# One-core graph network kernel: row moments on GpSimd, seven of eight tiles normalised on VectorE, and a reordered first row block

## The reference, cut to what matters

```
h  = relu(layernorm(x))
Wh = h @ W;  src = Wh @ a[:F];  dst = Wh @ a[F:]
att = softmax(where(adj > 0, leaky_relu(src + dst.T, 0.2), -9e15), axis=1)
x  = x + gru(att @ Wh, h)              # gates from w_ih, w_hh, b_ih, b_hh
h  = relu(layernorm(x))
out = x + adj @ (h @ W1.T + b1)
```

## Time and profile before

| | us |
|---|---|
| median of 3 runs | 1553.67 (1552.84 to 1554.71) |
| the profiled execution | 1554.47 |
| its span, first to last instruction | 1552.9 |
| TensorE busy | 1485.6 (96%) |
| VectorE busy | 1386.0 (89%) |
| ScalarE busy | 1369.6 (88%) |
| GpSimd busy | 136.2 (9%) |

### The profile page before, as it was taken

One profiled execution on the slowest core, in us unless ns is written; L12 is line 12 of the kernel. 1 busy time (PEld: TensorE's weight loads), 2 busy tenths in 40 slices (PEclk: granted clock), 3 DMA queues, 4 the chain that ended last, 5 costly groups with the idle time before them and its releaser, 6 DMA issues.

```text
span 1552.9 us, 35381 instructions
## 1 busy us (share of the span) xinstructions
PE 1485.6 (96%) x13262; PEld 1304.4 (84%) x13262; DVE 1386.0 (89%) x2256; ACT 1369.6 (88%) x1972; POOL 136.2 (9%) x98
## 2 busy tenths in 40 slices
PE   5477999999999999999999999999999999999998
PEld 5356888888888888888888888888888888888887
DVE  8997999999999999999999999997579877766684
ACT  5779999999999999999999999996185998777785
POOL 5000011001100010001000100010000000000000
PEclk9778999999999999999999999999999999999999
DMA  8858999999999999999999999996386999888860
GB/s 314 298 204 332 365 350 360 352 366 353 355 357 370 352 349 353 374 351 357 359 365 345 362 362 355 349 360 265 122 354 238 408 361 352 308 304 310 321 228 16
DMA packets 96380, 502.93 MB, mean 324 GB/s; under 512 B 9599, under 2 KB 38985, under 8 KB 75337
## 3 DMA queue, kind: packets, MB, share of 16 engines
q1 hardware_dynamic: 78328, 444.54, 76.1%
q10 hardware_dynamic: 18000, 57.74, 9.8%
HBM read 418.32 MB, written 83.92 MB: 323 GB/s over the span
## 4 chain that ended last, share of the span: by engine, by line
PE 92%; DVE 5%; ACT 1%; issue 1%; DMA 0%; POOL 0%; DVEq 0%; ACTq 0%
PE ACC L1014 57%; PE ACC L1104 29%; PE GP L1040 2%; PE GP L1043 2%; PE GQ L1061 1%; ACT M L506 1%; DVE M L659 1%; DVE JK L642 1%; DVE TB L733 1%; DVE AE L728 1%; DVE JK L728 1%; PE TG L1027 0%; PE TG L1050 0%; DVE JK L646 0%; DVE M L751 0%
## 5 line engine op out<-in xcount | busy, mean ns | idle before, releaser
L1014 PE MATMUL ACC<-TB,M 128*128 128x258 f16 x8192 | 927.2, 275 | 41.8 <-DVE M L751 30.7
L1014 PEld LDWEIGHTS ACC<-TB,M 128*128 128x128 fp8e4 x8192 | 804.5, 98 | 150.7 <-issue 43.2
L506 ACT ACTIVATE M<-SB,dsteep 128x256 fp8e4<-128x256 f32 x1273 | 526.2, 538 | 0.0
L516 ACT ACTIVATE JK<-X 128x3328 uint8<-128x3328 uint32 x124 | 373.2, 3010 | 0.0
L692 DVE TENSOR_SCALAR Y<-X 128x4096 fp8e4<-128x4096 f32 x128 | 291.9, 2280 | 5.9 <-DMA X<-in_adjb_dram 5.5
L605 ACT ACTIVATE TB<-TB 128x8192 uint8<-128x8192 fp8e4 x32 | 225.0, 7030 | 76.5 <-DVE TB L890 71.7
L1104 PE MATMUL ACC<-WG,X 128*128 128x256 f16 x2048 | 225.5, 273 | 0.0
L1104 PE MATMUL ACC<-WG,TB 128*128 128x256 f16 x2048 | 225.4, 273 | 0.0
L1104 PEld LDWEIGHTS ACC<-WG,X 128*128 128x128 fp8e4 x2048 | 200.4, 98 | 23.2
L1104 PEld LDWEIGHTS ACC<-WG,TB 128*128 128x128 fp8e4 x2048 | 200.4, 98 | 23.1
L743 DVE TENSOR_SCALAR M<-SB,nd 128x256 fp8e4<-128x256 f32 x775 | 213.7, 345 | 0.0
(11 more groups left out here) (145 smaller groups left out, 786.9 us busy)
## 6 DMA issues: line engine op xcount, KB each, us to landing
X<-in_adjb_dram SPq DMA_DIRECT2D x128, 2048.0 KB, 9.8
mask_bytes<-Y SPq DMA_DIRECT2D x128, 512.0 KB, 5.1
M<-in_adjb_dram ACTq DMA_DIRECT2D x24, 1920.0 KB, 9.8
X<-mask_bytes SPq DMA_DIRECT2D x16, 2048.0 KB, 9.5
TB<-mask_bytes SPq DMA_DIRECT2D x16, 2048.0 KB, 9.1
M<-in_adjb_dram ACTq DMA_DIRECT2D x4, 2048.0 KB, 11.9
M<-in_xb_dram SPq DMA_DIRECT2D x8, 512.0 KB, 8.3
h_rows<-M SPq DMA_DIRECT2D x8, 512.0 KB, 3.9
```

The costliest lines, as they stand in the source:

```text
L506: ins = nc.scalar.activation(rows(mask1(c), jj), SB[u][:, :], ACT.Sigmoid, scale=STEEP, bias=dsteep[:, j:j + 1], saturate=False)
L516: nc.scalar.activation(junk[:, 0:SEEN], X[c % 2][:, 0:SEEN].bitcast(u32), ACT.Sign, accum_out=nz[:, bass.ds(k, 1), at:at + 1].rearrange("p ...
L1014: ins = nc.tensor.matmul(A[t][m][:, 0:2 * TW], rows((mask1, mask2)[m](c), jj)[:, t * P:(t + 1) * P], TB[:, c * JC + jj, m, 0:2 * TW], star ...
```

## The change

Six edits, all at work before row block 1.

1. Row moments. VectorE aggregates only groups 0 and 1. For the others it runs `bn_stats` alone (`halves_stats`), and GpSimd's `pair_moments(p)` combines the two halves of each row's statistics for 16 tiles in seven small operations and raises to the power in an eighth. VectorE's order is now stats(0), stats(1), normalised(0), halves 2 and 3, the copy of `wext` that TensorE's first transposes wait for, normalised(1), halves 4 and 5, normalised(2), normalised(3), halves 6 and 7, normalised(4) to (7). GpSimd's pair 1 stands before the bias work, pairs 2 and 3 behind it.
2. BY_DVE is 7: VectorE normalises seven tiles of each group, ScalarE one.
3. GpSimd's weight work waits until VectorE has normalised everything (p_hd, 16).
4. X[0] is loaded after k = 11 and no longer after k = 7.
5. TSCALE goes into the exponent's bias as its logarithm; the two scalings (L720) fall away.
6. Row block 0. The low halves i = 3, 7, 11 and 15 are GpSimd's, with a semaphore t_lp of their own. ScalarE makes the first six comparisons (AHEAD) of the next part at the end of a part, so that behind the last high half of parts 1 to 3 only four comparisons stand and no longer ten.

The rest renumbers semaphores that are shared with these.

```diff
-BY_DVE = 6
+AHEAD = 6
+BY_DVE = 7
...
-                    if k in (7, 15):
+                    if k in (11, 15):
                         b = k // 15
                         sp.dma_start(X[b][:, :], adjb[b, :, :]).then_inc(c_in[b], 16)
...
+                def pair_moments(p):
...
+                    pool.wait_ge(p_st, 2 * p + 2)
+                    nc.gpsimd.tensor_tensor(px[0], mean_e, mean_o, ALU.add).then_inc(p_ag, 1)
+                    nc.gpsimd.tensor_tensor(px[1], part_e, part_o, ALU.add).then_inc(p_ag, 1)
+                    pool.wait_ge(p_ag, p * 6 - 5)
+                    nc.gpsimd.tensor_scalar(mean, px[0], 0.5, None, ALU.mult).then_inc(p_ag, 1)
+                    pool.wait_ge(p_ag, p * 6 - 4)
+                    nc.gpsimd.tensor_scalar(px[1], px[1], 1.0 / F, EPS, ALU.mult, ALU.add).then_inc(p_ag, 1)
+                    pool.wait_ge(p_ag, p * 6 - 3)
+                    nc.gpsimd.tensor_tensor(px[0], mean_e, mean, ALU.subtract).then_inc(p_ag, 1)
+                    pool.wait_ge(p_ag, p * 6 - 1)
+                    nc.gpsimd.tensor_tensor(px[0], px[0], px[0], ALU.mult).then_inc(p_ag, 1)
+                    pool.wait_ge(p_ag, p * 6)
+                    nc.gpsimd.tensor_tensor(sdx[:, at], px[1], px[0], ALU.add).then_inc(p_sd, 1)
+                    pool.wait_ge(p_sd, p + 2)
+                    nc.gpsimd.tensor_tensor(rsx[:, at], sdx[:, at], half[:, 0:1].to_broadcast([P, 16]), ALU.pow).then_inc(
+                        p_rs, 2)
+
-                for q in range(4):
+                for q in range(2):
                     deviation(q)
+                pair_moments(1)
...
-                for q in range(4, 8):
-                    deviation(q)
+                for p in range(2, 4):
+                    pair_moments(p)
+                pool.wait_ge(p_hd, 16)
                 pool.wait_ge(wt_in, 64)
...
+                for i in range(3, 16, 4):
+                    pool.wait_ge(t_hi, i + 1)
+                    j, m = i // 2 * 8, i % 2
+                    nc.gpsimd.tensor_tensor(TB[:, j:j + 8, m, TW:2 * TW], PB[i % 2], TB[:, j:j + 8, m, 0:TW],
+                                            ALU.subtract).then_inc(t_lp, 1)
...
+                def first_block(c):
+                    for i in range(4 * c, 4 * c + 2):
+                        table_high(i)
+                    if c == 0:
+                        act.wait_ge(p_nd, 2)
+                        act.wait_ge(p_hout, 128)
+                    first_masks(c, 0 if c == 0 else AHEAD, 6 if c == 0 else AHEAD + 6)
+                    for i in range(4 * c + 2, 4 * c + 4):
+                        table_high(i)
+                    first_masks(c, 6 if c == 0 else AHEAD + 6, JC)
+                    if c + 1 < CS:
+                        first_masks(c + 1, 0, AHEAD)
...
                 stats(0)
+                stats(1)
                 for q in range(8):
-                    if q < 7:
-                        stats(q + 1)
                     normalised(q)
+                    if q in (0, 1, 3):
+                        for ahead in range(q + q % 2 + 2, q + q % 2 + 4):
+                            halves_stats(ahead)
...
-                nc.vector.tensor_scalar(kt[:, 0:1], kt[:, 2:3], -1.0, None, ALU.mult)
+                nc.vector.tensor_scalar(kt[:, 0:1], kt[:, 2:3], -1.0, math.log(TSCALE), ALU.mult, ALU.add)
...
                 def table_product(i):
...
-                    wait(dve, t_lo, i - 1)
+                    if i < 2:
+                        dve.wait_ge(p_exp, i + 1)
+                    if i % 4 == 1:
+                        wait(dve, t_lp, i // 4)
+                    else:
+                        wait(dve, t_lo, (i - 2) // 4 * 3 + (i - 2) % 4 + 1 if i > 1 else 0)
...
                                     table_low(i)
-                                    table_low(i + 1)
+                                    if i % 4 == 0:
+                                        table_low(i + 1)
...
-                            pe.wait_ge(t_lo, 4 * (c + 1))
+                            pe.wait_ge(t_lo, 3 * (c + 1))
+                            pe.wait_ge(t_lp, c + 1)
```

More of the change, by code:

```diff
@@ L1 @@
 from contextlib import ExitStack
+import math
 import concourse.bass as bass
@@ L151, in binary_adjacency @@
         nmx = JK[:, 670:670 + NT]
+        px = [JK[:, 740 + 20 * i:740 + 20 * i + 16] for i in range(2)]
         BG = X1[0].bitcast(bf16)
@@ L206, in binary_adjacency @@
         d_hh, d_hl = sem("d_hh"), sem("d_hl")
+        t_lp = sem("t_lp")
+        p_ag = d_hh
         g_sum = p_wa
@@ L396, in deviation @@
                         p_rs, 1)
-                for q in range(4):
+                def pair_moments(p):
+                    at = slice(p * 16, p * 16 + 16)
+                    mean_e, part_e, mean_o, part_o = [stx[:, at, i:i + 1].rearrange("p t k -> p (t k)") for i in (1, 2, 4, 5)]
+                    mean = mvx[:, at, 0:1].rearrange("p t k -> p (t k)")
+                    pool.wait_ge(p_st, 2 * p + 2)
[15 more added lines that the diff above has]
+                for q in range(2):
                     deviation(q)
+                pair_moments(1)
                 pool.wait_ge(p_wa, 1)
@@ L490, in table_high, with first_masks @@
                     nc.scalar.activation(TB[:, j:j + 8, m, 0:TW], PB[i % 2], ACT.Copy).then_inc(t_hi, 1)
+                def first_masks(c, first, last):
+                    for jj in range(first, last):
+                        j = c * JC + jj
+                        ins = nc.scalar.activation(rows(mask1(c), jj), SB[0][:, :], ACT.Sigmoid, scale=STEEP,
+                                                   bias=dsteep[:, j:j + 1], saturate=False)
+                    if last == JC:
+                        ins.then_inc(c_ua, 1)
+                def first_block(c):
[10 more added lines that the diff above has]
+                        first_masks(c + 1, 0, AHEAD)
                 def sign_mask(g, u, k, c):
                     if c == 0:
[L494 to L499, removed]
+                        act.wait_ge(s_in[u], (k + u) * 16)
+                    act.wait_ge(c_pe, (g - 1) * CS + c + 1)
                     act.sem_inc(turn, 1)
                     for jj in range(first_on_act(g, c), JC):
-                        if isinstance(g, int) and g == 0 and jj == JC // 2 - 2:
-                            for i in range(4 * c + 2, 4 * c + 4):
-                                table_high(i)
                         j = c * JC + jj
@@ L512, in count @@
                     if isinstance(g, int) and g == 1 and c == 0:
-                        act.wait_ge(t_lo, 16)
+                        act.wait_ge(t_lo, 12)
+                        act.wait_ge(t_lp, 4)
                     wait(act, c_cnt, (g - 1) * CS + c)
@@ L564, in slot @@
                             if first:
-                                for i in range(4 * c, 4 * c + 2):
-                                    table_high(i)
-                            sign_mask(g, u, k, c)
+                                first_block(c)
+                            else:
+                                sign_mask(g, u, k, c)
                         if c == 0 and in_range(g, 2):
@@ L638, in _, with halves_stats @@
             def _(dve):
-                def stats(q):
+                def halves_stats(q):
                     dve.wait_ge(p_x[q], 16)
@@ L643, in stats @@
                     ins.then_inc(p_st, 1)
+                def stats(q):
+                    halves_stats(q)
                     dve.wait_ge(p_st, q + 1)
@@ L710, in _ @@
                 dve.wait_ge(p_k, 1)
-                nc.vector.tensor_scalar(kt[:, 0:1], kt[:, 2:3], -1.0, None, ALU.mult)
-                nc.vector.tensor_scalar(kt[:, 1:2], kt[:, 2:3], -SLOPE, None, ALU.mult).then_inc(p_k, 1)
+                nc.vector.tensor_scalar(kt[:, 0:1], kt[:, 2:3], -1.0, math.log(TSCALE), ALU.mult, ALU.add)
+                nc.vector.tensor_scalar(kt[:, 1:2], kt[:, 2:3], -SLOPE, math.log(TSCALE), ALU.mult, ALU.add).then_inc(p_k, 1)
                 nc.vector.tensor_scalar(sk, scol, kt[:, 2:3], 0.0, ALU.add, ALU.max).then_inc(p_sq, 1)
@@ L717, in table_product @@
                     if i == 0:
-                        for n, table in enumerate((bt, dt_)):
-                            dve.wait_ge(p_exp, n + 1)
-                            nc.vector.tensor_scalar(table, table, TSCALE, None, ALU.mult).then_inc(t_sc, 1)
                         dve.wait_ge(p_one, 2)
@@ L723, in table_product @@
                             dve.wait_ge(p_htout[b], 64)
-                        dve.wait_ge(t_sc, 2)
-                    wait(dve, t_lo, i - 1)
+                    if i < 2:
+                        dve.wait_ge(p_exp, i + 1)
+                    if i % 4 == 1:
+                        wait(dve, t_lp, i // 4)
+                    else:
+                        wait(dve, t_lo, (i - 2) // 4 * 3 + (i - 2) % 4 + 1 if i > 1 else 0)
                     j, m = i // 2 * 8, i % 2
@@ L822, in rows_step @@
                     if attending:
```

(2 more changed lines are left out.)

4 lines of the change are left out of this document (2 added, 2 removed).

## The result

| | us |
|---|---|
| before, median (8 runs on this chip) | 1553.26 (1552.71 to 1554.71) |
| after, median of 8 runs | 1558.13 (1557.42 to 1560.24) |
| ratio | 1.0029, 95% interval 1.0021 to 1.0038 |
| span, before and after | 1552.9 and 1557.3 |

The change costs 4.9 us by the medians and 4.4 us by the two spans. It is slower by more than 0.2%.

The account below looks back on a forecast made before the run. TensorE was taken as the bound, its last restart set by row block 0's last and. Stage one 2.0 us later plus row block 0 1.5 later made 3.5, so 1557.2 by the median; range 1549.5 to 1560.5.

Parts of the forecast that it names:

- What counts is the last and: Row block 0: the last and's start (103.89 us) sets when TensorE restarts for good; the stretch between them is fixed.
- Stage one on VectorE: Before the small chain: last tile done at 38 us, 4 us earlier, features(15) ready about 41.5.
- X[0]: First conversion: load issued at 35.9 lands at 44.9, so the small chain starts 2.0 us later.
- The scaling gives nothing: Exponentials before the first product: dropping the 0.49 us scaling gains nothing, as the first high half needs ScalarE anyway.
- Row block 0: Four parts before the last and: GpSimd's low half holds VectorE up, parts take 14.95 us, 1.5 us later in all.
- 1 (no shared port): Row block 0: GpSimd's low half costs VectorE nothing; 3.1 us earlier in all, 1550.6; chance 0.14.
- 2 (X[0] by 42.5): Stage one: X[0] lands by 42.5 because the queue is emptier; total 1554.8; chance 0.10.
- 3: Stage one and row block 0: free low half plus early X[0], or load no hindrance; 1548.2 or less; chance 0.06.
- 4 (TensorE waits for the low half): Row block 0: GpSimd loses the port at the and too, another 1 us a part; 1561 or more; chance 0.08.

Follow-up runs that it names:

- stage_one_only: Kernel after with row block 0 put back as before, keeping the changes to stage one and the exponents; median 1558.24, ratio 1.0031.
- late_x0: Kernel after with low halves on VectorE, X[0] loaded with X[1] behind half group 15 and converted in part 0; median 1551.98, ratio 0.9984.
- x0_early: Kernel after with X[0] loaded behind half group 7 again, not 11; median 1555.78, ratio 1.0009.
- low_on_vector: Kernel after with all low halves of row block 0 back on VectorE, comparisons ahead kept; median 1554.95, ratio 1.0002.

## Why the prediction was right

The forecast was 1557.2, range 1549.5 to 1560.5, slower; measured 1558.13. By its own steps:

- **What counts is the last and.** Right as to the path. That the stretch from the and to the restart is fixed was wrong: it was 21.64 and not 20.65 us from TensorE's start on. This is the step that failed. ScalarE's slack of 4.38 us was looked at, TensorE's own speed was not, though rows 3 had 9.11 us for 64 products that take 7.20 at the upper level later in the same trace. Missing from the sum are 1.0 in the last part and 0.5 behind the restart. Keeping TensorE busy takes the whole of the time at the lower level out, and the distance becomes 18.75.
- **Stage one on VectorE.** The last tile was forecast for 38 and was done at 37.1. The power over 16 values was forecast at 2.9 us and took 2.92 to 2.97. The wait for pair 3 was 1.13 for 0.8. Contention in the tiles was smaller: seven tiles took 2.54 and 2.12 us for 1.88 beside the bias work, 0.9 in sum for the 1.0 forecast, and 1.88 beside the moment operations of pairs 1 and 3, which cost nothing where 0.9 was set down. The features, forecast 3.2 us behind the last tile, came 5.1 behind it, at 42.2 for 41.5; X[0] hid this.
- **X[0].** Issued at 35.96 for the 35.9 forecast; 9.5 us to landing for 9.0; chain 2.6 us later for 2.0. The whole of the miss is the landing, inside the 8.1 to 10.3 of rows 9. By the 358 GB/s of the Trainium skill ("SBUF — State Buffer", section "A bandwidth-pool intuition that's wrong (but worth ruling out)") the estimate was 2.5, nearer than the rows' middle, for this one load. That is partly luck: the store ahead of it landed at 39.0 (issued at 35.47, 3.5 us) and not at 39.5, and the load 6.5 us behind it and not 5.9. stage_one_only shows that stage one carries the loss; late_x0, which keeps all of stage one but this wait, shows that the wait is the reason; and x0_early shows that loading X[0] earlier exchanges it for another.
- **The scaling gives nothing.** Right: the first product came 0.5 us sooner behind the chain's start, the first low half 0.08 (52.89 - 47.82 = 5.07 for 5.15), and VectorE waited 0.44 us for the high half.
- **Row block 0.** Mechanism right, size off: parts of 14.66 us for 14.95, 0.4 in all for 1.5. GpSimd held VectorE up for 1.88 us (3.10 - 1.22) and not 2.1: the subtraction of 1032 values took 1.9, where the line through 128 and 768 values gave 2.15. low_on_vector shows what that is worth: with the work back on VectorE a part is 0.74 shorter. The rule of the Trainium skill ("SBUF — State Buffer", section "Who interferes with whom"), that a two-operand VectorE instruction and a GpSimd one that reads SBUF exclude each other, agrees with the ands of 3.10 us, which no row of before had shown.
- **The near hit on the total** is partly chance: the block was 1.1 too dear, X[0] 0.6 too cheap, and the clock's 1.5 was missing.
- **Rivals.** 1 (no shared port) is refuted by the ands of 3.10. 2 (X[0] by 42.5) by the 8.48 us of waiting. 3 needs both. 4 (TensorE waits for the low half) didn't occur; no part of TensorE waits on GpSimd.

## What to carry to other kernels

Work taken from an engine is worth what its next instruction lets it be worth: look up what that instruction waits for, and which place in the queue lands it. Here moving a load behind waited-for stores and moving its use to where the engine was waiting anyway brought what offloading alone did not. An elementwise step handed from VectorE to GpSimd was paid here as serial time, because its neighbours on VectorE were a long conversion and an instruction that reads two operands; it saved 1.15 us and cost 1.88 a part. Where TensorE has gaps ahead of the point that sets the end, its own speed belongs in the sum.

## What was not expected of the hardware

- The granted clock of TensorE rose and fell through row block 0, and the same 64 products took 8.7 to 10.1 us by how much of them fell at the lower level; starts of the last part that were 1.4 and 3.1 us later made the span 0.8 and 3.2 us longer. Useless products of 0.163 us in the gaps held it at the upper level, gaps of 0.9 to 3.4 us included, and were worth 3.1 us.
- GpSimd lost the port to the conversion in all four parts when it subtracted, started within 0.04 us behind it, and won it in the run in which it only wrote, started within 0.02 us of it.
- GpSimd's scaling of 128x768 values took 2.14 us with VectorE idle. Before it took 2.13, though two of VectorE's tiles began and ended within it (by 38.51). In x0_early the conversion (38.27, 2.29 us, as long as ever) came 1.1 us behind its start, and the scaling took 1.95 us longer. So this instruction gives way to a conversion that comes later, and pays for it in time; the short tiles of before cost it none that shows.

```profile
37.15 4.09 POOL L445 TENSOR_SCALAR R<-R 128x768 f32<-128x768 f32 x1 [3.96 <-DVE M L711]
```
